# Perceiver layer on one core: V of all groups projected first and loaded back per group, and spare transposes in TensorE's waits

## The chip, the cores and the metric

One Trainium2 chip, one of its cores. The metric is the device time of one execution in microseconds (us), median of several. The engines are TensorE (PE, with its weight loads PEld), VectorE (DVE), ScalarE (ACT), GpSimd (POOL) and SyncE (SP), which here issues all DMAs.

## The reference

```python
# x: 128 x 512 (queries), ctx: 2048 x 512, mask all zeros
xn = layernorm(x)
q = rope((xn @ wq).heads(32)); k = rope((ctx @ wk).heads(8)); v = (ctx @ wv).heads(8)
# query heads 4g..4g+3 share key/value head g
x = x + softmax(q @ k.T / sqrt(128) + mask) @ v  (all heads joined) @ wo
x = x + mamba2(layernorm(x))       # 16 chunks of 512 inner columns, 8 norm groups
x = x + layernorm(x) @ dequant(w).T + bias
```

Only the first stage, cross attention, is rearranged. All data are float32.

## The kernel before

**Three products for one.** Each float32 operand of a large product is kept as a high part (rounded to fp32r) and a low part (the rest), and `pairs` issues three matmuls: high by high, high by low, low by high. ACT mostly makes the high parts (a copy), DVE or POOL the low parts (a subtraction). So each projected block costs a matmul group on TensorE and then one copy and one subtraction elsewhere.

**Groups.** The attention runs in 8 groups of one key/value head and four query heads (`with pe.Fori(0, G - 1)`, the last group written out behind the loop). In the loop body for group g TensorE computes: the scores of g, four heads of four blocks of 512 keys (`scores`); then for group g+1 the K blocks, Q and the first V block (`project_qk_and_first_v`); then `attend`, 16 steps t, each a transposition of the probabilities of 128 keys (`transpose_probs`, one transpose per head) and the product of an earlier step's transposed probabilities with V; then the output projection (`project_out`). The other V blocks of g+1 are placed inside and behind `attend`. A V block is projected as 128 head columns by 512 keys, so it must be copied out of its PSUM bank (`v_copy`) and transposed back by TensorE (`transpose_v_block`, four transposes) before `v_high` and `v_low` split it. That happens 32 times.

**Rotation.** K and Q pass through DVE's `k_rotate` and `q_rotate` (four instructions each: product with the cosine, two half products with the sine, sum), then ACT (`k_high`, `q_high`) and POOL or DVE (`k_low`, `q_low`). The transposed Q lies in `ring_b[0]` (PSUM bank 4) until `q_low` has read it. Step t of `attend` puts its transposes into `ring_b[(t + 1) % 2]`, so step 0 uses bank 5 and step 1 bank 4:

```python
if t == 1 and not last_head:
    pe.wait_ge(s["qT_lo_ready"], g + 2)
if t == 2 and not last_head:
    project_v_block(g + 1, 1)
```

**Order.** It is written by hand: each engine runs its own list and semaphores join them. Each engine's list is in strict order, SP's too. SP issues at the start the context (four blocks of 1 MB), the weights and rope tables of the first group, and the mask; in the loop, per group, `wo`, `wk`, `wv` and `wq`, where `wq` and `wo` share the buffer `wqo_raw` (`wq` of the next-but-one group is issued once `project_out` has finished). ACT splits both `wq` and `wo` (`wq_high`, `wo_high`), POOL subtracts (`wqo_low`). `exps` on ACT makes the probabilities, one instruction of 2048 columns per head, once `mask_scores` on DVE has masked the head's four blocks.

## Time and profile before

| quantity | value |
|---|---|
| median of 3 runs | 738.63 us (735.67 to 745.71) |
| the profiled execution | 734.99 us |
| its span, first to last instruction | 733.1 us |
| mean granted TensorE clock | 0.995 of full speed |

The durations below come from the profiled execution. Its own time is 1.9 us more than its span and 3.6 us under the median. Matmuls overlap in the records (one starts every 0.23 us and is shown with 0.39 us), so work on TensorE is counted from start to start.

### The profile page before, as it was taken

Reading aid. Unit: us, or ns where it says so; the run is one execution under the profiler, and the core shown is the slowest. Engines: PE = TensorE matmul, PEld = TensorE weight load, DVE = VectorE, ACT = ScalarE, POOL = GpSimd, SP = SyncE. Lnnn points to the kernel's source line nnn. Section 1 sums busy time; section 2 is a strip of 40 time slices with the busy share of each in tenths; the row PEclk is TensorE's granted clock in tenths of the full one; section 3 lists DMA queues with packets and bytes.
Section 4 is the critical chain, followed back from the end, with each engine's and each line's share of the span. In section 5 each row is a group of like instructions: output and inputs, shape, how many; then the busy total and the mean of one; then the engine's idle time right before and its main releaser. Section 6 shows DMA issues by size and latency. Waiting matters only on the chain.

```text
span 733.1 us, 11917 instructions
## 1 busy us (share of the span) xinstructions
PE 698.3 (95%) x3929; PEld 594.0 (81%) x3929; DVE 551.2 (75%) x1174; ACT 396.2 (54%) x602; POOL 300.6 (41%) x150
## 2 busy tenths in 40 slices
PE   5899999999999999999999999797979999999996
PEld 4678888888888888888888888686969998999985
DVE  5977658648848857765864874757999889998994
ACT  4364535536446446454553644653776666766752
POOL 3342404404503413230440440200268887888780
PEclk9999999999999999999999999999999999999999
DMA  9601021012001202202101200840897788787700
GB/s 321 244 26 72 1 72 57 14 47 80 16 12 59 72 0 72 72 0 72 57 14 56 72 0 0 316 175 4 311 329 305 285 321 317 294 330 303 276 25 15
DMA packets 20292, 93.74 MB, mean 128 GB/s; under 512 B 2609, under 2 KB 3761, under 8 KB 11441
## 3 DMA queue, kind: packets, MB, share of 16 engines
q1 hardware_dynamic: 20272, 93.50, 34.8%
q8 instruction: 10, 0.16, 0.1%
q14 instruction: 10, 0.07, 0.0%
HBM read 93.17 MB, written 0.33 MB: 128 GB/s over the span
## 4 chain that ended last, share of the span: by engine, by line
PE 87%; DVE 5%; DMA 4%; ACT 2%; issue 1%; SPq 0%; POOL 0%; POOLq 0%; DVEq 0%
PE bank L376 21%; PE bank L378 20%; PE bank L377 20%; PE bank L573 10%; PE bank L486 8%; PE bank L650 3%; PE bank L456 2%; DMA ctx_raw<-in_ctx_t 2%; DMA w_hs_sb<-in_w_hs 1%; DMA wqo_raw<-in_wo 1%; ACT probs L769 1%; PE bank L657 1%; PE bank L624 1%; PE bank L423 1%; DVE decay L1238 1%
## 5 line engine op out<-in xcount | busy, mean ns | idle before, releaser
L1395 POOL TENSOR_TENSOR wqo_lo<-wqo_raw,wqo_hi 128x2048 fp32r<-128x2048 f32 x15 | 69.5, 4632 | 207.1 <-ACT wqo_hi L705 175.6
L1070 DVE TENSOR_TENSOR pt_lo<-bank,pt_hi 128x512 fp32r<-128x512 f32 x128 | 87.7, 690 | 62.2 <-ACT pt_hi L779 62.2
L779 ACT ACTIVATE pt_hi<-bank 128x512 fp32r<-128x512 f32 x128 | 75.7, 598 | 66.0 <-PE bank L486 65.7
L1382 POOL TENSOR_TENSOR k_lo<-rope_a,k_hi 128x512 fp32r<-128x512 f32 x32 | 43.4, 1355 | 105.9 <-ACT k_hi L723 105.9
L1031 DVE CUSTOM_DVE_ANT_0 probs<-bank,mask_sb 128x512 f32<-128x512 f32 x128 | 82.2, 686 | 0.1
L486 PEld LDWEIGHTS bank<-ident,probs 128*128 128x128 f32 x512 | 63.6, 141 | 21.5 <-ACT probs L769 3.7
L486 PE MATMUL bank<-ident,probs 128*128 128x128 f32 x512 | 76.1, 274 | 4.6 <-ACT probs L760 3.3
L1425 POOL TENSOR_TENSOR w_out_lo<-w_out_sb,w_out_hi 128x2048 fp32r<-128x2048 f32 x16 | 73.4, 4587 | 17.2 <-ACT w_out_hi L880 17.2
L1430 POOL TENSOR_TENSOR w_gate_lo<-w_gate_sb,w_gate_hi 128x2048 fp32r<-128x2048 f32 x15 | 69.0, 4597 | 19.2 <-ACT w_gate_hi L872 19.2
L769 ACT ACTIVATE probs<-probs,neg_max 128x2048 f32<-128x2048 f32 x31 | 62.0, 2005 | 1.0 <-DVE neg_max L1021 0.6
L573 PE MATMUL bank<-xnT,w_hs_sb 128*128 128x128 f32 x512 | 59.7, 275 | 0.6 <-DMA w_hs_sb<-in_w_hs 0.6
L376 PE MATMUL bank<-pt_hi,v_hi 128*128 128x512 f32 x128 | 59.4, 464 | 0.0
L573 PEld LDWEIGHTS bank<-xnT,w_hs_sb 128*128 128x128 f32 x512 | 58.4, 192 | 0.8 <-DMA w_hs_sb<-in_w_hs 0.8
L1284 DVE SCALAR_TENSOR_TENSOR conv<-bank,cw,conv 128x127 f32<-128x127 f32 (+2 forms) x192 | 53.6, 341 | 4.3 <-DVE conv L1284 1.8
L723 ACT ACTIVATE k_hi<-rope_a 128x512 fp32r<-128x512 f32 x32 | 20.2, 632 | 64.4 <-DVE rope_a L982 64.4
L376 PE MATMUL bank<-ctx_hi,wk_hi 128*128 128x512 f32 x128 | 51.6, 403 | 1.1 <-DVE ctx_lo L1101 1.1
L376 PE MATMUL bank<-k_hi,qT_hi 128*128 128x512 f32 x128 | 51.4, 401 | 0.0
L376 PE MATMUL bank<-ctx_hi,wv_hi 128*128 128x512 f32 x128 | 51.2, 400 | 0.0
L378 PE MATMUL bank<-ctx_hi,wk_lo 128*128 128x512 f32 x128 | 50.9, 398 | 0.0
L377 PE MATMUL bank<-ctx_lo,wk_hi 128*128 128x512 f32 x128 | 50.8, 397 | 0.0
L378 PE MATMUL bank<-pt_hi,v_lo 128*128 128x512 f32 x128 | 50.7, 396 | 0.0
L377 PE MATMUL bank<-pt_lo,v_hi 128*128 128x512 f32 x128 | 50.4, 394 | 0.0
(186 smaller groups left out, 1709.4 us busy)
## 6 DMA issues: line engine op xcount, KB each, us to landing
w_hs_sb<-in_w_hs SPq DMA_DIRECT2D x16, 1024.0 KB, 4.8
w_gate_sb<-in_w_gate SPq DMA_DIRECT2D x16, 1024.0 KB, 4.8
w_out_sb<-in_w_out SPq DMA_DIRECT2D x16, 1024.0 KB, 6.4
wqo_raw<-in_wq SPq DMA_DIRECT2D x8, 1024.0 KB, 4.8
wqo_raw<-in_wo SPq DMA_DIRECT2D x8, 1024.0 KB, 4.8
decay<-decay_rows SPq DMA_DIRECT2D x16, 512.0 KB, 6.8
ctx_raw<-in_ctx_t SPq DMA_DIRECT2D x3, 1024.0 KB, 11.0
wk_raw<-in_wk SPq DMA_DIRECT2D x8, 256.0 KB, 2.7
```

Of the source, the lines that this page charges most:

```text
L376: pe.matmul(dst, left_hi, right_hi, start=first, stop=False)
L377: pe.matmul(dst, left_hi, right_lo, start=False, stop=False)
L378: return pe.matmul(dst, left_lo, right_hi, start=False, stop=last)
L486: last = pe.transpose(ring_b[(t + 1) % 2][:, h * P:(h + 1) * P], probs[:, h, t * P:(t + 1) * P], ident[:, :])
L573: last = pe.matmul(dst[:, t * P:(t + 1) * P], w[:, c, t * P:(t + 1) * P], xnT[:, c, :], start=c == 0, stop=c == KC - 1)
L769: act.activation(probs[:, h, :], probs[:, h, :], ACT.Exp, bias=neg_max[:, h:h + 1], accum_out=row_sum[:, h:h + 1]).then_inc(s["probs_ready ...
L779: act.activation(pt_hi[t % 3], ring_b[(t + 1) % 2][:, :], ACT.Copy).then_inc(s["pt_hi_ready"], 1)
L1031: dve.tensor_tensor_reduce(out=probs[:, h, b * 512:(b + 1) * 512], in0=ring_a[b][:, :], in1=mask_sb[:, b * 512:(b + 1) * 512], scale=1.0, ...
L1070: dve.tensor_tensor(pt_lo[t % 3], ring_b[(t + 1) % 2][:, :], pt_hi[t % 3].bitcast(F32), ALU.subtract)\
L1395: pool.tensor_tensor(wqo_lo[:, :, :], wqo_raw[:, :, :], wqo_hi[:, :, :].bitcast(F32), ALU.subtract)\
L1425: pool.tensor_tensor(w_out_lo[:, i, :, :], w_out_sb[:, i, :, :], w_out_hi[:, i, :, :].bitcast(F32), ALU.subtract).then_inc(s["wout_lo_read ...
L1430: pool.tensor_tensor(w_gate_lo[:, i, :, :], w_gate_sb[:, i, :, :], w_gate_hi[:, :, :].bitcast(F32), ALU.subtract).then_inc(s["gate_lo_read ...
```

## The change

- **V first.** Before the loop, V of all eight groups is projected as 32 tiles (`project_v`): 128 keys by the columns of four groups, with the context as the stationary operand, so no transposition is needed. The tile goes through ACT (`v_high`) and DVE (`v_low`) into `pt_hi`/`pt_lo`, two slots, and SP stores both parts to DRAM (`store_v`). A slot is free for tile t+2 once its store has landed (`v_out`).
- **V per group.** `load_v` brings 2 MB, high and low, for each group: for group 0 in the middle of the projection, later when the previous group's `attend` has ended. `wv` arrives in two halves of four groups (`wva`, `wvb`), each as four DMAs that write pieces of 128 columns.
- **The loop** loses all V projections, V copies and V transposes. The scores of a group's head 0 move ahead of `project_out` of the group before. K block 3 moves into `attend` at t = 2, its rotation is spread over steps 3, 5, 7 and 9 (`ROPE_STEPS`), and its `k_high` stands behind step 11. The order of the rotation's steps changes: sines first, then the cosine product in PSUM, then a sum that reads PSUM.
- **Splits.** `wo` is split on POOL (`split_wo`) instead of ACT and POOL. `wq_high` of the next group stands behind the first head's exponential.
- **Spare transposes** (`turn_identity`): 32 and 14 at the start, 28 before and 13 behind the last `attend`, 26 and 6 around the second norm, 12, 13 and 12 in the second stage.

```diff
+            for h in range(HG):
+                sp.dma_start(wva_raw[:, :, h * DH:(h + 1) * DH], wv[h]).then_inc(s["wva_in"], 16)
             load_context(1)
...
+            sp.wait_ge(s["ctx_lo_ready"], 4)
+            for h in range(HG):
+                sp.dma_start(wvb_raw[:, :, h * DH:(h + 1) * DH], wv[HG + h]).then_inc(s["wvb_in"], 16)
+
+            def store_v(tile):
+                half, t = tile // KT, tile % KT
+                sp.wait_ge(s["v_lo_ready"], tile + 1)
+                for store, part in zip(v_store, (pt_hi, pt_lo)):
+                    sp.dma_start(store[half, t, :, :], part[tile % 2].bitcast(F32)).then_inc(v_out[tile % 2], 16)
+
+            def load_v(half, h):
+                for store, part in zip(v_store, (v_hi, v_lo)):
+                    sp.dma_start(part[:, :, :].bitcast(F32), store[half, :, :, h * DH:(h + 1) * DH].rearrange("t p d -> p t d"))\
+                        .then_inc(s["v_in"], 16)
...
+                sp.wait_ge(s["pv_ready"], g + 1)
+                load_v((g + 1) // HG, (g + 1) % HG)
+                sp.wait_ge(s["oproj_ready"], g + 1)
+                if g + 2 < G:
+                    sp.dma_start(wqo_raw[:, :, :], wq[g + 2]).then_inc(s["wq_in"], 16)
...
+            def turn_identity(count, spare):
+
+                for _ in range(count):
+                    pe.transpose(spare[:, 0:P], ident[:, :], ident[:, :])
...
+            def project_v(tile):
+                t = tile % KT
+                if tile < KT:
+                    right_hi, right_lo = wva_hi, wva_lo
+                else:
+                    right_hi, right_lo = wvb_hi, wvb_lo
+                    pe.wait_ge(s["wvb_lo_ready"], 1)
+                if tile >= 2:
+                    pe.wait_ge(s["v_lo_ready"], tile - 1)
                 for c in range(KC):
...
+            for b in range(KB):
+                project_k_block(0, b)
+                for t in range(4):
+                    project_v(4 * b + t)
+            for t in range(KT):
+                if t == KT // 2:
+                    project_q(0)
+                if t == 3 * KT // 4:
+                    transpose_q(0)
+                project_v(KT + t)
+            scores(0, range(1))
             with pe.Fori(0, G - 1) as g:
-                scores(g)
-                project_qk_and_first_v(g + 1)
+                scores(g, range(1, HG))
+                project_k_block(g + 1, 0)
+                project_k_block(g + 1, 1)
+                project_q(g + 1)
+                project_k_block(g + 1, 2)
+                transpose_q(g + 1)
                 attend(g, False)
-                transpose_v_block(g + 1, 0)
-                project_v_block(g + 1, 3)
-                transpose_v_block(g + 1, 1)
+                scores(g + 1, range(1))
                 project_out(g)
-                transpose_v_block(g + 1, 2)
-            scores(G - 1)
+            scores(G - 1, range(1, HG))
+            turn_identity(28, bank[4])
             attend(G - 1, True)
+            turn_identity(13, bank[4])
...
+            def v_high(tile):
+                act.wait_ge(s["v_mm"], tile + 1)
+                if tile >= 2:
+                    act.wait_ge(v_out[tile % 2], 32 * (tile // 2))
+                act.activation(pt_hi[tile % 2], v_bank[tile % 2][:, :], ACT.Copy).then_inc(s["v_hi_ready"], 1)
...
             with dve.Fori(0, G - 1) as g:
-                mask_scores(g)
-                q_and_k(g + 1)
+                mask_scores(g, range(1, HG))
+                k_rotate(g + 1, 0)
+                k_rotate(g + 1, 1)
+                q_rotate(g + 1)
+                k_rotate(g + 1, 2)
+                q_low(g + 1)
                 pt_low(g, False)
                 scale_out(g)
-                v_low(g + 1, 0)
                 attn_low(g)
-                v_low(g + 1, 1)
+                mask_scores(g + 1, range(1))
                 add_out(g)
-                v_low(g + 1, 2)
```

**DVE in the loop, between the rotation of Q and the first `pt_lo`.** Bank 7 holds Q, banks 1 and 2 the K blocks 1 and 2, bank 4 the transposed Q. Before:

```order
L991 TENSOR_TENSOR rope_a<-bank7,cos_q 128x512 [waits qproj_ready]
L993 SCALAR_TENSOR_TENSOR rope_b<-bank7,sin_q 128x4x64
L994 TENSOR_TENSOR rope_b<-bank7,sin_q 128x4x64
L996 TENSOR_TENSOR rope_a<-rope_a,rope_b 128x512 [waits qrope_mul]
L969 REGISTER_ALU
L977 TENSOR_TENSOR rope_a<-bank1,cos_k 128x512 [waits qT_mm,kproj_ready]
L978 TENSOR_TENSOR rope_b<-bank1,sin_k 64x512
L979 TENSOR_TENSOR rope_b<-bank1,sin_k 64x512
L982 TENSOR_TENSOR rope_a<-rope_a,rope_b 128x512 [waits krope_mul]
L1001 TENSOR_TENSOR qT_lo<-bank4,qT_hi 128x512 [waits qT_hi_ready]
```

With the change:

```order
L1012 SCALAR_TENSOR_TENSOR rope_b<-bank7,sin_q 128x4x64 [waits k_lo_ready,qproj_ready]
L1013 TENSOR_TENSOR rope_b<-bank7,sin_q 128x4x64
L1015 TENSOR_TENSOR bank7<-bank7,cos_q 128x512 [waits qrope_sin]
L1019 TENSOR_TENSOR rope_a<-bank7,rope_b 128x512 [waits qrope_mul]
L983 REGISTER_ALU
L988 TENSOR_TENSOR rope_b<-bank2,sin_k 64x512 [waits k_lo_ready,kproj_ready]
L990 TENSOR_TENSOR rope_b<-bank2,sin_k 64x512
L994 TENSOR_TENSOR bank2<-bank2,cos_k 128x512 [waits krope_sin]
L998 TENSOR_TENSOR rope_a<-bank2,rope_b 128x512 [waits krope_mul]
L1024 TENSOR_TENSOR qT_lo<-bank4,qT_hi 128x512 [waits qT_hi_ready]
```

The rotation of K block 1 moved ahead of Q's, and the rotation of block 2 now stands between Q's rotation and `qT_lo`.

**TensorE in the loop, at the start of `attend`.** Before, the last matmuls of V block 0 (bank 0) stand in front:

```order
L378 MATMUL bank0<-ctx_hi,wv_lo 128x512
L486 MATMUL bank5<-ident,probs 128x128 [waits v_lo_ready,probs_ready]
L486 MATMUL bank5<-ident,probs 128x128 x3
L486 MATMUL bank4<-ident,probs 128x128 [waits qT_lo_ready]
L486 MATMUL bank4<-ident,probs 128x128 x3
```

With the change:

```order
L417 MATMUL bank2<-ctx_hi,wk_lo 128x512
L464 MATMUL bank4<-ident,rope_a 128x128 [waits qrope_add]
L464 MATMUL bank4<-ident,rope_a 128x128 x3
L500 REGISTER_ALU
L506 MATMUL bank5<-ident,probs 128x128 [waits probs_ready]
L506 MATMUL bank5<-ident,probs 128x128 x3
L506 MATMUL bank4<-ident,probs 128x128 [waits qT_lo_ready]
L506 MATMUL bank4<-ident,probs 128x128 x3
L415 MATMUL bank3<-ctx_hi,wk_hi 128x512 [waits scores_masked]
```

Only the transposes of step 0 stand between the transposes of Q and those that need `qT_lo`; before, K blocks 2 and 3 and V block 0 stood there too.

**SP, in the middle of the V projection**, where the last tile of the first half is stored and V of group 0 loaded. With the change (nothing of this stands before):

```order
L317 DMA v_high<-pt_hi 128x512 [waits v_lo_ready]
L317 DMA v_low<-pt_lo 128x512
L327 DMA wk_raw<-in_wk 128x512 [waits kproj_ready]
L321 DMA v_hi<-v_high 128x16x128 [waits v_out1,v_out0]
L321 DMA v_lo<-v_low 128x16x128
L317 DMA v_high<-pt_hi 128x512 [waits v_lo_ready]
```

The two loads of 1 MB stand in the queue ahead of the next tile's store.

## Rows read from the trace of the kernel before

**Rows 1.** The page: busy time per engine, and the chain that ended last.
```profile
PE 698.3 (95%) x3929; PEld 594.0 (81%) x3929; DVE 551.2 (75%) x1174; ACT 396.2 (54%) x602; POOL 300.6 (41%) x150
...
PE 87%; DVE 5%; DMA 4%; ACT 2%; issue 1%; SPq 0%; POOL 0%; POOLq 0%; DVEq 0%
```
**Rows 2.** Windows (PE, PEld, DVE, ACT, POOL, clock, DMA, GB/s); the second is one loop body.
```profile
24.00:43.00 19.00, 17.93 (x87) 14.83 (x85) 13.65 (x17) 7.24 (x11) 7.62 (x5) 1.00 0.38 144
180.80:240.30 59.50, 59.47 (x304) 49.14 (x303) 41.49 (x86) 29.79 (x41) 18.09 (x11) 1.00 0.14 45
476.00:492.00 16.00, 15.35 (x86) 12.72 (x87) 9.86 (x19) 9.09 (x19) 0.00 (x0) 0.90 0.54 205
506.00:516.00 10.00, 10.00 (x78) 10.00 (x77) 9.10 (x26) 4.25 (x11) 0.00 (x0) 0.83 0.30 88
```
**Rows 3.** Timeline of PE around one V block's transposes (start, duration).
```profile
214.60 0.60 PE L456 MATMUL bank<-ident,rope_b 128*128 128x128 f32 x4
214.96 0.48 PE L376 MATMUL bank<-ctx_hi,wv_hi 128*128 128x512 f32 x1
215.27 0.39 PE L377 MATMUL bank<-ctx_lo,wv_hi 128*128 128x512 f32 x1
```
**Rows 4.** Timeline of PE: first matmul of K block 0, Q and K block 1.
```profile
232.88 0.39 PE L376 MATMUL bank<-ctx_hi,wk_hi 128*128 128x512 f32 x1
...
235.59 0.40 PE L376 MATMUL bank<-wqo_hi,qx_hi 128*128 128x512 f32 x1
...
238.39 0.39 PE L376 MATMUL bank<-ctx_hi,wk_hi 128*128 128x512 f32 x1
```
**Rows 5.** Timeline of DVE, the rotations that follow.
```profile
235.79 0.69 DVE L977 TENSOR_TENSOR rope_a<-bank,cos_k 128x512 f32<-128x512 f32 x1 [1.72 <-PE bank L378]
...
238.59 0.69 DVE L991 TENSOR_TENSOR rope_a<-bank,cos_q 128x512 f32<-128x512 f32 x1
239.20 0.41 DVE L993 SCALAR_TENSOR_TENSOR rope_b<-bank,sin_q 128x256 f32<-128x256 f32 x1
...
244.83 0.68 DVE L1001 TENSOR_TENSOR qT_lo<-bank,qT_hi 128x512 fp32r<-128x512 f32 x1
```
**Rows 6.** Timeline of PE at the start: cold matmuls, and the wait for the first Q.
```profile
9.31 0.63 PE L377 MATMUL bank<-ctx_lo,wk_hi 128*128 128x512 f32 x1
9.74 0.63 PE L378 MATMUL bank<-ctx_hi,wk_lo 128*128 128x512 f32 x1
...
23.55 0.66 PE L423 MATMUL bank<-ident,rope_a 128*128 128x128 f32 x4 [3.46 <-DVE rope_a L996]
```
**Rows 7.** DMA issues: count, size of one, us from issue to landing.
```profile
wqo_raw<-in_wq SPq DMA_DIRECT2D x8, 1024.0 KB, 4.8
wk_raw<-in_wk SPq DMA_DIRECT2D x8, 256.0 KB, 2.7
mask_sb<-in_mask SPq DMA_DIRECT2D x1, 1024.0 KB, 11.8
dtb_bc<-in_dt_bias SPq DMA_DIRECT2D x1, 64.0 KB, 12.1
alog_bc<-in_a_log SPq DMA_DIRECT2D x1, 64.0 KB, 12.8
```
**Rows 8.** Timeline of SP's queue: three issues.
```profile
16.62 0.55 SPq L288 DMA_DIRECT2D mask_sb<-in_mask  x1
...
462.90 0.49 SPq L323 DMA_DIRECT2D dtb_bc<-in_dt_bias  x1
463.43 0.46 SPq L323 DMA_DIRECT2D alog_bc<-in_a_log  x1
```
**Rows 9.** Timeline: ACT and POOL on wq in the loop.
```profile
226.13 1.92 ACT L705 ACTIVATE wqo_hi<-wqo_raw 128x2048 fp32r<-128x2048 f32 x1 [0.66 <-DMA wqo_raw<-in_wq]
...
228.12 4.64 POOL L1395 TENSOR_TENSOR wqo_lo<-wqo_raw,wqo_hi 128x2048 fp32r<-128x2048 f32 x1 [28.11 <-ACT wqo_hi L705]
```
**Rows 10.** Timeline of PE: the last group's wait.
```profile
474.27 1.07 PE L486 MATMUL bank<-ident,probs 128*128 128x128 f32 x8 [3.34 <-ACT probs L760]
```

More of the change, by code:

```diff
@@ L227, in build @@
         same_step_bank = bank[7]
+        v_bank = [bank[5], bank[6]]
+        v_store = [nc.dram_tensor(f"v_{part}", (G // HG, KT, P, HG * DH), F32).ap() for part in ("high", "low")]
         decay_rows = nc.dram_tensor("decay_rows", (CH, HC * P), F32).ap()
@@ new lines, in load_v @@
+            def load_v(half, h):
+                for store, part in zip(v_store, (v_hi, v_lo)):
+                    sp.dma_start(part[:, :, :].bitcast(F32), store[half, :, :, h * DH:(h + 1) * DH].rearrange("t p d -> p t d"))\
+                        .then_inc(s["v_in"], 16)
+            for tile in range(KT):
+                store_v(tile)
+            sp.wait_ge(s["kproj_ready"], KB)
+            sp.dma_start(wk_raw[:, :, :], wk[1]).then_inc(s["wk_in"], 16)
+            for slot in range(2):
+                sp.wait_ge(v_out[slot], 32 * KT // 2)
@@ L462, in scores @@
+            def scores(g, heads):
                 pe.wait_ge(s["qT_lo_ready"], g + 1)
-                for h in range(HG):
+                for h in heads:
                     for b in range(KB):
@@ L645, in chunk_step @@
                     hs_step(1, 0)
+                elif isinstance(n, int) and n == 0:
+                    turn_identity(13, bank[6])
                 pe.wait_ge(s["x_ready"], c + 1)
@@ L654, in chunk_step @@
                     out_step(n + i - 1, 1 - i)
+                if first or last_chunk:
+                    turn_identity(12, bank[1] if last_chunk else bank[3])
                 pe.wait_ge(s["y_gated"], c + 1)
@@ L764, in exps @@
                 for h in range(HG):
+                    if h == 1 and not last_head:
+                        wq_high(g + 1)
                     act.wait_ge(s["neg_max_ready"], HG * g + h + 1)
@@ L783, in pt_high @@
                         act.activation(probs[:, 2, 0:512], oq_bank[:, :], ACT.Copy).then_inc(s["bcast_ready"], 1)
-                if not last_head:
-                    v_copy(g + 1, 1)
+                    if t == 11 and not last_head:
+                        k_high(g + 1, KB - 1)
             def ctx_high(b, pieces=slice(0, KC)):
@@ L797, in _ @@
             ctx_high(0, PAIRS[1])
-            act.wait_ge(s["wq_in"], 16)
-            for two, done in zip(PAIRS, (s["first_wq_hi"], s["wq_hi_ready"])):
-                act.activation(wqo_hi[:, two, :], wqo_raw[:, two, :], ACT.Copy).then_inc(done, 1)
+            act.wait_ge(s["wva_in"], 64)
+            for two in PAIRS:
+                act.activation(wva_hi[:, two, :], wva_raw[:, two, :], ACT.Copy).then_inc(s["wva_hi_ready"], 1)
             act.wait_ge(ctx_in[1], 16)
@@ L1022, in row_max, with mask_scores @@
                     .then_inc(s["neg_max_ready"], 1)
-            def mask_scores(g):
-                for h in range(HG):
+            def mask_scores(g, heads):
+                for h in heads:
                     for b in range(KB):
@@ L1075, in pt_low @@
                         inverse_sums_low(g)
+                    if not last_head and t in ROPE_STEPS:
+                        k_rotate_step(g + 1, KB - 1, ROPE_STEPS.index(t))
             def scale_out(g):
@@ L1120, in _ @@
             ctx_low(1, 3, PAIRS[0])
+            v_low(0)
             ctx_low(1, 4, PAIRS[1])
+            v_low(1)
             first_k_rotate(0)
+            v_low(2)
+            ctx_low(2, 5)
+            v_low(3)
+            v_low(4)
+            first_k_rotate(1)
+            v_low(5)
+            ctx_low(3, 6)
+            for tile in range(6, 9):
+                v_low(tile)
+            first_k_rotate(2)
+            for tile in range(9, 13):
+                v_low(tile)
+            first_k_rotate(3)
@@ L1410, in _ @@
             split_wk(0)
-            split_wv(0)
-            k_low(0)
+            k_low(0, range(1))
+            for c in range(KC):
+                pool.wait_ge(s["wq_hi_ready"], 1)
+                last = pool.tensor_tensor(wqo_lo[:, c, :], wqo_raw[:, c, :], wqo_hi[:, c, :].bitcast(F32), ALU.subtract)
+            last.then_inc(s["wq_lo_ready"], 1)
+            k_low(0, range(1, 2))
+            for c in range(KC):
+                pool.wait_ge(s["wvb_hi_ready"], 1)
+                last = pool.tensor_tensor(wvb_lo[:, c, :], wvb_raw[:, c, :], wvb_hi[:, c, :].bitcast(F32), ALU.subtract)
+            last.then_inc(s["wvb_lo_ready"], 1)
+            k_low(0, range(2, KB))
             with pool.Fori(1, G) as g:
```

330 lines of the change are left out of this document (140 added, 190 removed).

## The prediction

> **What bounds the kernel now.** I read the page first: TensorE is busy for 95% of the span and holds 87% of the chain that ended last [rows 1]. Then the windows: a loop body of one group takes 59.5 us, of which TensorE is busy 59.47 at the full clock, DVE 41.5, ACT 29.8, POOL 18.1; DMA engines are busy 14% [rows 2]. In the loop every matmul taken away counts fully, as long as nobody makes TensorE wait. The timelines then give the prices. The waits outside the loop are few: 3.46 us for the first rotated Q [rows 6], 3.34 us before the last group's transposes [rows 10], and short ones around the norms. I make the sum against the profiled execution's own 734.99 us (span 733.1), which is 3.6 us under the median of 738.63.
>
> **What goes.** The V matmuls do not go: 32 blocks of 12 before, 32 tiles of 12 now, all of 512 columns. They only move ahead of the loop: 12 take 2.71 us from start to start [rows 4]. Only the transposes go. Four of them and the slower start of the next matmul take 215.27 - 214.60 = 0.67 us where one matmul takes 0.23, so 0.44 us per block, and 32 x 0.44 = **-14.1 us** [rows 3]. ACT's copies of V (32) and DVE's and ACT's V splits leave the loop; they were hidden, so they pay nothing by themselves. A loop body without stalls would take 59.5 - 4 x 2.71 - 4 x 0.44 = 46.9 us.
>
> **The start.** The first matmuls run 0.43 us apart against 0.23 later, that is at the 1.2 GHz level; about 14 of them cost 2.8 us, and Q is now needed much later, so the wait of 3.46 us goes as well [rows 6]. Against that the spare transposes (32, then 14) may hold TensorE for longer than the norm does, and V tile 0 must wait for 1 MB more of weights, split by ACT and DVE. I take **-4 us** (0 to -6).
>
> The Trainium skill (TensorE: Matmul & The Clock Gate, "The HAM clock gate") says that the clock rises only with sustained work, which makes spare transposes in a wait useful. The trace agrees in part: the stretch after the 3.34 us wait has a mean granted clock of 0.90, while the stretch behind the 3.46 us wait has 1.00 throughout [rows 2]. By the page alone both long waits would be followed by cold matmuls; the trace shows that a wait of this length sometimes is and sometimes is not.
>
> **Wait A, the first stores.** Tile 2 needs slot 0, which is free when tile 0's store has landed, and TensorE's tile 4 needs `v_lo` of tile 2. The stores stand behind all loads on one queue. Before, the mask landed at 16.6 + 11.8 = 28.4 us [rows 7, 8], and 9 MB were through by then (0.33 MB/us). Now 0.8 MB more come before the mask's end and `wvb` (1 MB) behind it: 28.4 + 5.5 = 34 us, or 39 us if DMAs with pieces of 512 bytes take twice their time (2 MB of them). The store itself lands 2.7 us after it gets its turn, as a load of 256 KB does, and ACT and DVE need 1.4 us. So tile 4 may start at 37 to 42 us. TensorE gets there earlier: tile 0 at about 15, four tiles and K block 1, 5 x 2.71, makes 28.5. The wait is 9 to 13 us, and the next matmuls may start cold (up to 2.8 us): **+13 us**. In steady state a slot needs 0.7 + 0.7, one further issue of 0.5 [rows 8] and 2.7, 4.6 us, and two tiles give it 5.4, so stores are otherwise hidden, by less than a microsecond.
>
> **Wait B, loading V of group 0.** On SP both loads of 1 MB stand between the stores of tiles 15 and 16. Tile 16's store lands later by the loads' time L, and there are about 2 us of slack. What L is, no row shows: the pieces are 512 bytes. Full rate (0.33 MB/us) gives 6 us. The far end is the row of 64 KB loads with 512 bytes per partition: two of them, issued at 462.90 and 463.43, land at 475.0 and 476.2, so 1.2 us for 64 KB and 39 us for 2 MB [rows 7, 8]. That includes each DMA's own overhead, so it is far too dear for two large ones; I stay near the first end and take L = 11 us. Two microseconds of this lie beside the wait for the landing itself. The wait is 1 to 30 us; I take **+5 us**.
>
> The Trainium skill (DMA: Bandwidth & Descriptors, "Specifications") gives 512 bytes as the smallest transfer at line rate. By that rule L is 6 us and the loads cost next to nothing anywhere; no row here shows large transfers in such pieces.
>
> **The loop: a new wait at step 1 of `attend`.** Let K block 0 start at 0. TensorE: K0 to 2.71, K1 to 5.42, Q (2.80) to 8.22, K2 to 10.93, transposes of Q and step 0 (0.44 each) to 11.8, then the transposes of step 1, which overwrite the bank that `qT_lo` reads. DVE: starts 0.20 after K0's end (235.79 - 235.59), at 2.91; a rotation takes 238.59 - 235.79 = 2.80 [rows 4, 5]. K0 to 5.71, K1 to 8.51, Q to 10.7 (two halves at 0.33 and 0.45, two full ones at 0.7), then K2 is only ready at 11.13 and is done at 13.93, and only then `qT_lo` (0.68): 14.6. TensorE goes on at 14.75 instead of 11.8. Before, K blocks 2 and 3 and V block 0 (8.1 us of matmuls) stood in between, and `qT_lo` came ahead of block 2's rotation. So **+2.9 us per group, 7 x 2.9 = +20.3 us** (0 only if DVE ran much faster than in these rows; it has no reason to). In steps 3 to 9 DVE does 1.4 us in some steps of 1.13; the slack of the two-step distance and of K block 3 takes it, with up to 0.5 us per group left over. If TensorE falls to the lower level after the wait, up to 2.4 us per group come on top.
>
> **The loop: wq behind V.** `load_v` is issued when `attend` ends, `wq` 5.5 us later behind it on the queue. From `attend`'s end to the next Q are 2.71 + 2.80 + 3 x 2.71 + 2 x 2.71 = 19.1 us. `wq` needs, from its turn, 2.7 to 4.8 us to land, 1.9 on ACT and 4.6 on POOL [rows 7, 9]: about 10. So L may be 9 us before Q waits; at 11 it waits 2 us, and every further microsecond counts seven times. ACT waits for `wq` too, with the exponentials of heads 1 to 3 (6 us) and then `k_high` behind it, which gives the same delay or a little more. I take **+1.5 us per group, +10.5 us** (0 to 90). The other queued work has room: `wo` on POOL (a copy and a subtraction of 4.6 us) is done long before `project_out`; `attn_lo` follows the last product by three operations of 0.7 us, and the scores of head 0 cover 2.7.
>
> **The end.** Exponentials of the last group no longer stand behind `wo`'s copy, so 3.34 us shrink, but 28 spare transposes (0.11 each, 3.1 us) fill the same place: about -0.3. The clock stays up there (0.90 over 16 us before, so 3.2 us at the lower level) and behind the second norm (0.83 over 10 us, 3.4 us at it); half of each is lost time [rows 2]. The other spare transposes fit waits of their length. **-3.5 us** (-4 to +2).
>
> **Sum:** -14.1 - 4 + 13 + 5 + 20.3 + 10.5 - 3.5 = +27.2. 734.99 + 27 = **762 us**.
>
> **The rivals.**
> 1. *DMA is hidden, the DVE wait is not.* Pieces of 512 bytes run at full rate, A is 9 us, B 1, wq 0: -14.1 - 4 + 9 + 1 + 20.3 - 3.5 = +8.7, 744 us. For it: the DMA engines idle for 86% of a loop body [rows 2]. Against: the stores' landing time bounds A whatever the rate.
> 2. *Faster.* Both long new waits are absent or mostly covered: the stores overtake the backlog, and DVE reaches `qT_lo` in time. Then -14.1 - 4 + 1 + 0 + 2 - 3.5 = -18.6, 716 us. For it: TensorE is the bound and really loses work. Against: the order on DVE, and one queue for all.
> 3. *V's loads are slow.* L = 15 to 20: Q waits 6 to 11 us per group, B grows to 10: 762 + 7 x 4.5 + 5 = 799 us and up to 840. This decides from L = 9 us on. For it: the 1.2 us rows. Against: they price small DMAs.
> 4. *The spare transposes do nothing* beyond their place (the waits were too short to cool the engine): only the -3.5 and part of the start go, +5 us on any of these.
>
> **How the numbers follow.** My case, both waits with L around 11: 0.40, 750 to 785. Rival 1: 0.25. Rival 2: 0.18. Rival 3: 0.17. Faster or slower by over 2% is about what a measurement of this kernel tells from no change: below 724 or above 753 us. Rival 2 is mostly below; of rival 1 most is within 2% and some above; my case is above but for a tenth, rival 3 all above. Faster 0.16, same 0.25, slower 0.59. The range leaves out the upper part of rival 3 and the lower of rival 2: 717 to 800.
>
> **What would show it.** Right: no `L456` work and TensorE's V matmuls in one stretch of about 90 us; a PE idle of 9 us or more between tiles 3 and 4, at 28 to 40 us, released by `pt_lo`; the waits table with seven waits of some 2.9 us of the transposes for `qT_lo`; loop periods of 50 to 52 us; DMA writes of 16 MB. Wrong: periods under 48 us (DVE was in time), or the V stretch under 92 us from tile 0 to tile 31 (stores never held it); periods over 54 us with ACT waiting for `wqo_raw` is rival 3.

## The result: 771.33 us, 4.4% slower

Before takes 740.17 us (median of 4 runs beside the new one, 735.67 to 745.71), the changed kernel 771.33 us (4 runs, 768.93 to 772.12). The ratio is 1.0435, 95% interval 1.0387 to 1.0484. The prediction of 762 us has the side right and is 9 us short. Its sum was made against the profiled execution of 734.99 us; the profiled one of after takes 770.9 us, span 769.2. So the trace has +36 us to explain where the sum had +27.

The page of after, in the same order as [rows 1], with the line of the granted clock in 40 slices between:

```profile
PE 719.1 (93%) x3957; PEld 606.8 (79%) x3957; DVE 547.5 (71%) x1174; ACT 368.2 (48%) x564; POOL 308.5 (40%) x150
...
PEclk9889999999999999999999999999999999999999
...
PE 68%; issue 14%; DVE 8%; DMA 3%; POOL 3%; SPq 2%; ACT 1%; POOLq 0%; DVEq 0%; ACTq 0%
```

TensorE is busy 20.8 us longer than before. The transposes of V that are gone (19.0 us in the table of groups) and the 156 turns that came (21.1 us) nearly cancel, so the same matmuls ran slower. TensorE's part of the chain that ended last fell from 87% to 68%. DVE, POOL and SP's queue gained 2 to 3 points each, and most of the rest is "issue", time for which the page names no wait, so the shares alone don't say who is to blame. The waits of PE, in total, times and longest:

```profile
PE bank L506 <- DVE qT_lo L1024: 18.7, 7, 2.7
PE bank L415 <- DVE pt_lo L1030: 16.5, 5, 9.4
...
PE bank L415 <- DVE wva_lo L1133: 1.3, 1, 1.3
```

These are the two kinds that the prediction named: seven times `qT_lo` in the loop, and in the V stretch five for `pt_lo`, which there is the low part of a V tile. The windows of after, with the columns of [rows 2]: the matmuls behind the first long wait, then two loop bodies, then the stretch around the wait inside the second of them.

```profile
39.30:44.60 5.30, 5.28 (x12) 4.13 (x13) 2.77 (x2) 2.28 (x2) 2.95 (x3) 0.50 0.52 198
...
159.90:211.70 51.80, 48.99 (x239) 39.50 (x238) 38.34 (x81) 23.45 (x32) 18.07 (x9) 0.97 0.28 86
211.70:263.00 51.30, 48.62 (x239) 39.58 (x238) 38.25 (x81) 23.46 (x32) 18.07 (x9) 0.97 0.28 86
...
211.70:220.30 8.60, 5.93 (x26) 4.78 (x25) 5.76 (x11) 2.31 (x4) 4.71 (x3) 0.80 0.19 82
```

The granted clock is 0.97 in each loop body, and the last row shows where it is lost: in the 8.6 us around the wait it is 0.80, and in the other 42.7 us of that body it is 1.00. A loop body takes 51.8 us the first time and 51.3 on average later, against 59.5 before [rows 2]. The prediction had 46.9 for one without stalls. PE in the second of them:

```profile
211.72 0.60 PE L464 MATMUL bank<-ident,rope_a 128*128 128x128 f32 x4
212.16 0.60 PE L506 MATMUL bank<-ident,probs 128*128 128x128 f32 x4
215.42 1.11 PE L506 MATMUL bank<-ident,probs 128*128 128x128 f32 x4 [2.67 <-DVE qT_lo L1024]
216.19 0.77 PE L415 MATMUL bank<-ctx_hi,wk_hi 128*128 128x512 f32 x1
216.76 0.63 PE L416 MATMUL bank<-ctx_lo,wk_hi 128*128 128x512 f32 x1
217.19 0.63 PE L417 MATMUL bank<-ctx_hi,wk_lo 128*128 128x512 f32 x1
...
218.89 0.40 PE L415 MATMUL bank<-ctx_hi,wk_hi 128*128 128x512 f32 x1
...
220.28 0.60 PE L506 MATMUL bank<-ident,probs 128*128 128x128 f32 x4
```

Three things are to be read here. The wait is 2.67 us. Behind it the starts lie 0.43 us apart (216.76, 217.19), which is the 1.2 GHz level, until 218.9; at 2.4 GHz they lie 0.23 apart [rows 4]. And step 2 starts 4.86 us after step 1, where four transposes and K block 3 need 3.26 at the full clock (run c). From the first group to the last this distance shrinks from 4.83 and 4.86 to 4.62. DVE in the same stretch shows why the wait is there:

```profile
211.92 0.69 DVE L988 TENSOR_TENSOR rope_b<-bank,sin_k 64x512 f32<-64x512 f32 x1 [0.45 <-PE bank L417]
...
214.08 0.69 DVE L998 TENSOR_TENSOR rope_a<-bank,rope_b 128x512 f32<-128x512 f32 x1
214.69 0.68 DVE L1024 TENSOR_TENSOR qT_lo<-bank,qT_hi 128x512 fp32r<-128x512 f32 x1
```

Four operations of K block 2's rotation, two of them in the part left out, stand ahead of `qT_lo`. ACT had its input ready at 212.96.

The V stretch. SP's queue (issue and its duration), then ACT, which has to wait for the slot, then PE:

```profile
21.23 9.37 SPq L311 DMA_DIRECT2D wvb_raw<-in_wv  x4
30.65 2.44 SPq L317 DMA_DIRECT2D v_high<-pt_hi  x1
```

```profile
37.95 0.60 ACT L753 ACTIVATE pt_hi<-bank 128x512 fp32r<-128x512 f32 x1 [8.42 <-DMA v_low<-pt_lo]
```

```profile
39.32 0.79 PE L415 MATMUL bank<-wva_hi,ctx_hi 128*128 128x512 f32 x1 [9.36 <-DVE pt_lo L1030]
...
99.52 0.76 PE L415 MATMUL bank<-wvb_hi,ctx_hi 128*128 128x512 f32 x1 [5.01 <-DVE pt_lo L1030]
100.08 0.63 PE L416 MATMUL bank<-wvb_lo,ctx_hi 128*128 128x512 f32 x1
100.50 0.63 PE L417 MATMUL bank<-wvb_hi,ctx_lo 128*128 128x512 f32 x1
```

The first row is tile 4, the second tile 20. The loads of V, which had no row before, and `wq` beside [rows 7]:

```profile
wqo_raw<-in_wq SPq DMA_DIRECT2D x8, 1024.0 KB, 6.4
v_high<-pt_hi SPq DMA_DIRECT2D x32, 256.0 KB, 2.1
v_low<-pt_lo SPq DMA_DIRECT2D x32, 256.0 KB, 2.4
v_hi<-v_high SPq DMA_DIRECT2D x8, 1024.0 KB, 5.8
v_lo<-v_low SPq DMA_DIRECT2D x8, 1024.0 KB, 9.1
```

`wq` is in time, but only just. ACT waits for its landing, POOL's subtraction follows, and Q's first matmul follows that. The first round, then POOL in the second:

```profile
199.37 1.92 ACT L732 ACTIVATE wqo_hi<-wqo_raw 128x2048 fp32r<-128x2048 f32 x1 [2.69 <-DMA wqo_raw<-in_wq]
201.37 4.64 POOL L1427 TENSOR_TENSOR wqo_lo<-wqo_raw,wqo_hi 128x2048 fp32r<-128x2048 f32 x1 [17.07 <-ACT wqo_hi L732]
206.07 0.50 PE L415 MATMUL bank<-wqo_hi,qx_hi 128*128 128x512 f32 x1
...
252.51 4.63 POOL L1427 TENSOR_TENSOR wqo_lo<-wqo_raw,wqo_hi 128x2048 fp32r<-128x2048 f32 x1 [16.38 <-ACT wqo_hi L732]
```

In the first round POOL ends at 206.01 and Q starts at 206.07, 0.28 us later than the matmuls ahead of it would allow. In the second POOL ends at 257.14 and Q starts on time at 257.58. In the later rounds the margin is 0.25 to 0.54 us.

The last group's wait of [rows 10] is filled with turns and then over:

```profile
508.42 3.22 PE L422 MATMUL bank<-ident 128*128 128x128 f32 x28
511.47 1.04 PE L506 MATMUL bank<-ident,probs 128*128 128x128 f32 x8
```

### The profile page after: what moved, and what is told of

Same layout as the page of the kernel before. It is cut to its first block, busy times and chain, and to the rows that moved or that the text cites. A ratio compares the mean times of both kernels' runs of the same rounds, so it can differ in the third digit from the quotient of the medians.

```text
span 769.2 us, 11882 instructions
## 1 busy us (share of the span) xinstructions
PE 719.1 (93%) x3957; PEld 606.8 (79%) x3957; DVE 547.5 (71%) x1174; ACT 368.2 (48%) x564; POOL 308.5 (40%) x150
## 3 DMA queue, kind: packets, MB, share of 16 engines
q1 hardware_dynamic: 65584, 127.06, 46.9%
## 4 chain that ended last, share of the span: by engine, by line
PE 68%; issue 14%; DVE 8%; DMA 3%; POOL 3%; SPq 2%; ACT 1%; POOLq 0%; DVEq 0%; ACTq 0%
PE bank L415 16%; PE bank L416 15%; PE bank L417 15%; PE bank L596 9%; PE bank L506 7%; PE bank L675 3%; POOL wqo_lo L1427 1%; SPq L311 1%; DMA w_hs_sb<-in_w_hs 1%; DMA wva_raw<-in_wv 1%; PE bank L422 1%; DVE bank L994 1%; DVE rope_b L990 1%; DVE rope_b L988 1%; PE bank L684 1%
## 5 line engine op out<-in xcount | busy, mean ns | idle before, releaser
L1083 DVE TENSOR_TENSOR pt_lo<-bank,pt_hi 128x512 fp32r<-128x512 f32 x128 | 87.9, 691 | 57.7 <-ACT pt_hi L780 57.3
L780 ACT ACTIVATE pt_hi<-bank 128x512 fp32r<-128x512 f32 x128 | 76.4, 597 | 84.6 <-PE bank L506 84.2
L1414 POOL TENSOR_TENSOR k_lo<-rope_a,k_hi 128x512 fp32r<-128x512 f32 x32 | 41.2, 1287 | 159.8 <-ACT k_hi L746 159.8
L506 PE MATMUL bank<-ident,probs 128*128 128x128 f32 x512 | 80.5, 281 | 20.1 <-DVE qT_lo L1024 18.7
L1427 POOL TENSOR_TENSOR wqo_lo<-wqo_raw,wqo_hi 128x2048 fp32r<-128x2048 f32 x7 | 32.5, 4639 | 157.6 <-ACT wqo_hi L732 157.6
L506 PEld LDWEIGHTS bank<-ident,probs 128*128 128x128 f32 x512 | 63.4, 144 | 39.2 <-DVE qT_lo L1024 20.3
L1030 DVE TENSOR_TENSOR pt_lo<-bank,pt_hi 128x512 fp32r<-128x512 f32 x32 | 22.1, 691 | 78.0 <-ACT pt_hi L753 78.0
L753 ACT ACTIVATE pt_hi<-bank 128x512 fp32r<-128x512 f32 x32 | 19.1, 596 | 75.8 <-PE bank L417 51.5
L415 PE MATMUL bank<-ctx_hi,wk_hi 128*128 128x512 f32 x128 | 54.5, 426 | 0.9 <-DVE ctx_lo L1116 0.8
L416 PE MATMUL bank<-ctx_lo,wk_hi 128*128 128x512 f32 x128 | 53.3, 416 | 0.0
L416 PE MATMUL bank<-k_lo,qT_hi 128*128 128x512 f32 x128 | 50.0, 390 | 0.0
```

The lines of the kernel that those rows point to most:

```text
L415: pe.matmul(dst, left_hi, right_hi, start=first, stop=False)
L416: pe.matmul(dst, left_hi, right_lo, start=False, stop=False)
L506: last = pe.transpose(ring_b[(t + 1) % 2][:, h * P:(h + 1) * P], probs[:, h, t * P:(t + 1) * P], ident[:, :])
L780: act.activation(pt_hi[t % 3], ring_b[(t + 1) % 2][:, :], ACT.Copy).then_inc(s["pt_hi_ready"], 1)
L1083: dve.tensor_tensor(pt_lo[t % 3], ring_b[(t + 1) % 2][:, :], pt_hi[t % 3].bitcast(F32), ALU.subtract)\
```

## The experiments

Each median is to be held against after (771.33) or before (about 740); each ratio is to the runs of before on the same chip, with its 95% interval.

### a. `qT_lo` ahead of K block 2's rotation

```diff
                 q_rotate(g + 1)
+                q_low(g + 1)
                 k_rotate(g + 1, 2)
-                q_low(g + 1)
                 pt_low(g, False)
```

> One edit in VectorE's loop: qT_lo is made ahead of the rotation of K block 2. With K block 0 started at 0, Q is rotated at about 10.9 us, transposed at 11.4, copied by ACT at 12.1 and qT_lo is done at about 12.9, where TensorE arrives at 11.8: the wait of 2.67 us shrinks to about 1.1. Theory (each of the seven waits costs its own 2.67 us and then about 2.2 us at the lower clock): if a wait of 1.1 us doesn't lower the clock, the period falls from 51.8 to about 48.0 us and the kernel to about 744 us; if it does, to about 50.2 us and 760 us. Rival (the lower clock after the wait is no loss of its own, the period is set by DVE anyway): only 1.6 us per group go, 760 us at a full clock.

Measured: 758.7 us, 1.0295 (1.0221 to 1.037). PE in its second group:

```profile
214.66 0.66 PE L506 MATMUL bank<-ident,probs 128*128 128x128 f32 x4 [0.97 <-DVE qT_lo L1024]
...
219.50 0.63 PE L506 MATMUL bank<-ident,probs 128*128 128x128 f32 x4 [1.44 <-DVE pt_lo L1083]
```

The wait fell to 0.97 us as computed, and the clock stayed up (K block 3's starts are 0.23 apart). But the rotation, moved behind, delayed `pt_lo` of step 0, and step 2 now waits 1.44 us. The period is 49.8 us. So neither figure of the theory was met by its own way: 12.6 us came back rather than 27, because the work that stood in the way had only changed its place. The rival's number (760 us at a full clock) fits, and so does half of its reason: DVE still holds TensorE for 0.97 + 1.44 = 2.41 us per group where it was 2.67. Its other half, that the lower clock costs nothing, doesn't fit: the waits lost 0.26 us per group and the period 1.5. Run c tests that by itself.

### b. K block 3 ahead of step 1

```diff
                     if t == 1 and not last_head:
+                        project_k_block(g + 1, KB - 1)
                         pe.wait_ge(s["qT_lo_ready"], g + 2)
-                    if t == 2 and not last_head:
-                        project_k_block(g + 1, KB - 1)
```

> One edit on TensorE: K block 3 is projected ahead of step 1 of attend instead of ahead of step 2. Its 2.71 us stand where the wait of 2.67 us was. Theory: the wait goes altogether and with it the lower clock behind it; step 2 may wait 0.3 us for pt_lo of step 0. Period 46.9 to 47.4 us, 7 x 4.6 = 32 us less than 770.9: 737 to 742 us. Rival (DVE is what holds the group: its work, 38 us of a period, is delayed by the same amount wherever TensorE waits): the wait moves to step 2 or 3, the period stays above 50 us, 758 us or more.

Measured: 747.33 us, 1.0151 (1.0068 to 1.0234).

```profile
212.96 0.66 PE L506 MATMUL bank<-ident,probs 128*128 128x128 f32 x4
214.32 0.63 PE L506 MATMUL bank<-ident,probs 128*128 128x128 f32 x4 [0.71 <-DVE pt_lo L1082]
```

Step 1 no longer waits, the clock is full, 0.71 us of waiting is left at step 2, and the period is 48.0 us. One order on one engine is worth 24 us. The theory's mechanism holds, its size was 5 us too good: 0.71 us of waiting where it had 0.3, a body without stalls that takes 47.2 us and not 46.9 (run c), and in the first round a Q 0.93 us late for `wq`, whose margin went with the longer wait.

### c. The wait kept, but filled

```diff
                     if t == 1 and not last_head:
+                        turn_identity(23, oq_bank)
                         pe.wait_ge(s["qT_lo_ready"], g + 2)
```

> The wait for qT_lo stays, but TensorE fills it with 23 turns of the identity (2.6 us). Theory (of the 4.9 us that a group takes over its unstalled 46.9, 2.67 are the wait and 2.2 the lower clock after it): the period falls from 51.8 to about 49.6 us, the kernel to about 755 us, and the mean granted clock of a period rises from 0.97 to 1.00. Rival (the lower clock costs nothing of its own, since DVE paces the steps after the wait): period 51.8 us, 771 us, unchanged though the clock is full.

Measured: 759.37 us, 1.0304 (1.0229 to 1.0379).

```profile
212.60 2.67 PE L422 MATMUL bank<-ident 128*128 128x128 f32 x23
215.43 0.66 PE L506 MATMUL bank<-ident,probs 128*128 128x128 f32 x4 [0.15 <-DVE qT_lo L1025]
...
218.69 0.60 PE L506 MATMUL bank<-ident,probs 128*128 128x128 f32 x4
```

Compare with the rows of after above. Step 1 starts at 215.43 here and 215.42 there, so DVE holds it just as long. Step 2 follows after 3.26 us here and 4.86 there: in this group 1.60 us are the lower clock and nothing else. In the seven groups of after the excess over 3.26 is 1.57, 1.60, 1.49, 1.42, 1.37, 1.36 and 1.36 us, 10.2 in all. The spans of the two profiled executions differ by 10.3 us, the medians by 12.0. The rival is out. The theory's 2.2 us per group was too much, as a body without stalls takes 47.2 us: 49.9 here less the 2.7 that the turns fill, or 51.3 - 2.67 - 1.44 in after.

### d. No turns at all

```diff
-                for _ in range(count):
+                for _ in range(0):
```

> All turns of the identity left out (they feed no result). From the profiles of before and after, the tail from the last scores to the end took 262.2 us before and 260.8 now, and the start some 2.8 us less. Theory: the turns at the start save about 2.8 us of the lower clock, those in the tail 1.4 us, and elsewhere nothing: 775 us. Rival 4 of the prediction (they do nothing): 771 us; a third reading, that they themselves delay the work behind them: below 770 us.

Measured: 771.25 us, 1.0498 (1.0406 to 1.059), by the medians the same as after. The start shows where the gain goes. PE, K block 0 and V tile 0 without turns:

```profile
10.90 0.76 PE L415 MATMUL bank<-ctx_hi,wk_hi 128*128 128x512 f32 x1 [3.50 <-DVE ctx_lo L1116]
...
16.16 0.48 PE L415 MATMUL bank<-wva_hi,ctx_hi 128*128 128x512 f32 x1
```

and with them, in after:

```profile
11.07 0.47 PE L415 MATMUL bank<-ctx_hi,wk_hi 128*128 128x512 f32 x1 [0.83 <-DVE ctx_lo L1116]
...
15.70 0.50 PE L415 MATMUL bank<-wva_hi,ctx_hi 128*128 128x512 f32 x1 [1.33 <-DVE wva_lo L1133]
```

With the turns K block 0 runs at the full clock, and TensorE then waits 1.33 us for the weights of V. Tile 4 starts at 39.07 without and 39.32 with them: the first store decides, not the clock. In the profiled executions the turns are worth 0.8 us by the rotated Q of group 1 (159.91 with, 160.75 without) and 0.4 us behind the last loop body, and against that the first wait for `qT_lo` was followed by the full clock without the turns (1.6 us) and by the lower clock with them. So rival 4 of the prediction holds for this kernel to within a microsecond or two.

### e. First stores ahead of the second half's weights

```diff
-            sp.wait_ge(s["ctx_lo_ready"], 4)
-            for h in range(HG):
-                sp.dma_start(wvb_raw[:, :, h * DH:(h + 1) * DH], wv[HG + h]).then_inc(s["wvb_in"], 16)
...
             for tile in range(KT):
                 store_v(tile)
+                if tile in (2, 4, 6, 8):
+                    h = tile // 2 - 1
+                    sp.dma_start(wvb_raw[:, :, h * DH:(h + 1) * DH], wv[HG + h]).then_inc(s["wvb_in"], 16)
```

ACT's copy of `wvb` moves behind tile 11, POOL's subtraction behind K block 2.

> The four loads of wvb (9.4 us of issue in the profile of after) are taken from their place ahead of the first store of V and issued one by one behind the stores of tiles 2, 4, 6 and 8; ACT and POOL split wvb later to match. Theory (the first store is late because it is issued behind these loads): the store of tile 0 is issued at about 22 us, lands at 25 to 29, and TensorE's wait of 9.36 us ahead of tile 4 with the 2.5 us of lower clock behind it shrinks to 0 to 2 us: 10 to 12 us less, 759 to 762 us. Rival (it is the backlog of bytes of context, tables and mask that holds the store, not the issues behind it): the store lands at 33 us or later, the wait is 5 us or more, 766 us or more.

Measured: 766.88 us, 1.0357 (1.0272 to 1.0443).

```profile
20.29 0.53 SPq L314 DMA_DIRECT2D v_high<-pt_hi  x1
```

```profile
34.10 0.60 ACT L753 ACTIVATE pt_hi<-bank 128x512 fp32r<-128x512 f32 x1 [5.48 <-DMA v_low<-pt_lo]
```

```profile
35.48 0.80 PE L415 MATMUL bank<-wva_hi,ctx_hi 128*128 128x512 f32 x1 [6.41 <-DVE pt_lo L1031]
```

The store is issued 10.4 us earlier than in after and lands only 3.9 us earlier, 13.2 us after the issue of its second half. Its bytes stand in the queue behind context, tables and mask. The rival is right in the main: about 6.4 of the 9.4 us are the backlog, 3 are `wvb`. The median fell by 4.5 us, 1.5 more than the wait shrank. In the profiled execution the first wait for `qT_lo` was followed by the full clock here too, which is worth 1.6 us; whether that is so in the other runs is not on record.

### f. V of group 0 loaded behind the last store

```diff
-            for slot in range(2):
-                sp.wait_ge(v_out[slot], 32 * KT // 2)
-            load_v(0, 0)
             for tile in range(KT, 2 * KT):
                 store_v(tile)
...
             for slot in range(2):
                 sp.wait_ge(v_out[slot], 32 * KT)
+            load_v(0, 0)
```

> V of group 0 is loaded behind the last store of V instead of between the stores of tiles 15 and 16. Theory (the store of tile 16 lands late because two loads of 1 MB stand ahead of it): the wait of 5.01 us ahead of tile 18 falls to below 1 us, with the 1.7 us of lower clock behind it, and the load lands some 10 us after the last store, at about 150, well before step 2 of attend at 166: 6 us less, 765 us. Rival (the wait comes from the state of the queue, or the load is needed earlier): unchanged at 771 us, or a new wait for v_hi at step 2.

Measured: 760.34 us, 1.0291 (1.0205 to 1.0377). (The expectation names tile 18; the wait is ahead of tile 20.) PE's waits for the low part of V:

```profile
PE bank L413 <- DVE pt_lo L1028: 11.9, 4, 9.7
```

The 5.01 us are gone, and there is no wait for `v_hi`. By the rotated Q of group 1 this kernel is 8.8 us ahead of after (151.14 against 159.91). Of these 2.0 are there by tile 7 (48.97 against 50.98), where the two kernels are still the same, so 6.8 belong to wait B: its 5.01 and the 1.7 of slow matmuls behind it. By group 2 it is 10.7 us ahead, since `wq` of the first round no longer comes 0.28 us late and the first wait of the loop was followed by no lower clock (1.00 over the first round). The whole is 11 us, of which wait B is the larger part and not all.

### g. The turns alone, in the kernel before

The same turns at the same places of the kernel before (the 28 in `pv_bank`), and nothing else.

> The kernel before with nothing of the V change, only with the turns of the identity at the same places (32, 14, 28, 13, 26, 6, 13, 12 and 12). Theory (they keep the clock up where TensorE waits, but what comes behind waits for data anyway): the start saves up to 2.8 us, the tail up to 1.4: 0 to 4 us less, ratio 0.995 to 1.000. Rival: all of the lower clock of these stretches is real loss and comes back, 5 us or more, ratio 0.993 or less.

Measured: 734.88 us, 0.9937 (0.9897 to 0.9977). In the kernel before the turns bring 5 us, 0.6%, and the interval lies below 1. The ratio lies between the theory's (0.995 or more) and the rival's (0.993 or less), nearer the rival's, and the interval covers both. The granted clocks on record point at the same cause: their median is 0.995 over these ten runs and 0.988 over the thirteen of before beside them. At half speed where it is low, 0.7% of 735 us is an estimate of 5 us. In which stretches they arise isn't settled: the profiled execution took 737.66 us, 2.7 more than that of before, and so does not show them.

### h. `wq` ahead of V in the queue

```diff
-                sp.wait_ge(s["pv_ready"], g + 1)
-                load_v((g + 1) // HG, (g + 1) % HG)
                 sp.wait_ge(s["oproj_ready"], g + 1)
                 if g + 2 < G:
                     sp.dma_start(wqo_raw[:, :, :], wq[g + 2]).then_inc(s["wq_in"], 16)
+                sp.wait_ge(s["pv_ready"], g + 1)
+                load_v((g + 1) // HG, (g + 1) % HG)
```

on top of b.

> K block 3 ahead of step 1 as in the run b_k3_early, and on the queue wq of the next group ahead of the loads of V. Theory (the wait of 0.77 us of Q for wqo_lo there is the load of V ahead of wq, the prediction's term of +1.5 us per group, hidden only behind the longer wait in after): it goes, 7 x 0.7 = 5 us less than b_k3_early, 742 us; V's load then lands later, still before step 2. Rival (wq is bound by its own issue after project_out, ACT and POOL, not by the load ahead of it): the same 747 us.

Measured: 748.93 us, 1.0128 (1.0047 to 1.0209), the same as b. The wait of 0.77 us that the expectation speaks of came once in b, in the first round, and not seven times; here it is gone, and the period is 48.0 us in both. The load of V ahead of `wq` takes that one wait and otherwise only margin: ACT's idle time for `wq` falls from 13.4 us in b to 4.6.

### k. Edits b, e and f together

> K block 3 ahead of step 1, stores of V ahead of the wvb loads, and V of group 0 loaded behind the last store, together. Theory (the three losses are independent, and only the wait behind the backlog of loads is left): from 771.3, minus 24.0, 4.5 and 11.0 as measured alone, gives 732 us, ratio about 0.99. Rival (they share a cause, one wait moves into another's place): 740 us or more.

Measured: 736.22 us, 0.9965 (0.9933 to 0.9998). 35 us of the expected 39.5 came back. Part of the difference is probably counted twice in the expectation: the profiled executions of e and f each had a first round without the lower clock (1.6 us), and b takes that lower clock away as well. So the losses are nearly independent.

### j. k, with the first four stores on ACT's queue

```diff
             v_high(0)
+            store_first_v(0)
```

and so behind tiles 1 to 3, where `store_first_v(t)` waits for `v_lo_ready` and issues both stores with `act.dma_start`.

> As k_three_edits, but the stores of tiles 0 to 3 are issued by ACT on its own queue instead of by SP behind the loads of context, tables and mask. Theory (these stores wait in SP's queue for the bytes ahead of them): they land about 3 us after their issue at 20 us, the wait of 6.4 us ahead of tile 4 shrinks to 2 us or less and with it 1.7 to 2.5 us of lower clock: 6 to 8 us under k_three_edits, 724 to 726 us. Rival (the DMA engines themselves are full until 33 us, whichever queue asks): the wait stays at 5 to 6 us, and the time within 2 us of k_three_edits.

Measured: 734.02 us, 0.9928 (0.9901 to 0.9954). PE's waits in the V stretch, here and then in k:

```profile
PE bank L416 <- DVE pt_lo L1040: 5.8, 6, 1.7
```

```profile
PE bank L413 <- DVE pt_lo L1028: 8.7, 4, 6.5
```

The longest wait shrank from 6.5 to 1.7 us, without a lower clock behind it, and group 2 is reached 4.0 us earlier (194.58 against 198.55). The rest then took 1.4 us more, and the medians differ by 2.2, with intervals that overlap. The store of tile 1 still took over 8 us here (issued at 25.13 and 25.49, ACT goes on at 34.15), so a queue of its own shortens the way past a backlog and does not remove it. The DMA engines were full: their share is 0.96 or more until 36 us.

The Trainium skill (DMA: Bandwidth & Descriptors, "Queues, rings and completion order") says that each DMA engine serves the queues that have work in turn, packet by packet, and each queue's ring in order. Both halves agree with e and j: 13.2 us behind the backlog in SP's queue, and under 9 us (34.15 - 25.49) beside it.

### l. ACT copies step 0 ahead of K block 2

```diff
                 q_high(g + 1)
-                k_high(g + 1, 2)
                 pt_high(g, False)
...
+                    if t == 0 and not last_head:
+                        k_high(g + 1, 2)
```

on top of j.

> j_act_queue with one edit on ACT: the probabilities of step 0 are copied ahead of the last copy of K block 2 instead of behind it. In b_k3_early DVE waited 0.58 us for that copy, and TensorE 0.71 us for pt_lo at step 2. Theory (this order is what is late there): the seven waits of 0.71 us go, the period falls from 48.0 to about 47.4 us, 4 us less than j_act_queue: 730 us. Rival (DVE reaches pt_lo late anyway, behind the rotation of K block 2): the wait stays, 734 us.

Measured: 733.66 us, 0.9934 (0.9899 to 0.9968), the same as j.

```profile
202.67 0.66 PE L507 MATMUL bank<-ident,probs 128*128 128x128 f32 x4 [0.33 <-DVE pt_lo L1094]
```

Steps 1 and 2 start without a wait, and step 4 waits 0.33 us instead. The period is 48.0 (48.2 in j). Neither reading is quite right: the order on ACT was what step 2 waited for, but removing it pays nothing. TensorE now waits for DVE's `pt_lo` two steps later; DVE has `pt_lo`, the inverse sums, the diagonals and a rotation in the first steps, and that it is the slower one there was not tried by itself. The time is the rival's.

### m. Three slots for V tiles

Tiles 0 to 23 take turns in three slots, the third being `qT_hi` and `qT_lo`; the rest is l.

> l_act_order with three slots instead of two for V tiles on their way to memory (the third is the place of qT_hi and qT_lo, free until tile 24). Theory (each tile waits for the landing of the store two tiles back, with less than 1 us of slack): the six waits for pt_lo in the V stretch, 5.8 us in all in j_act_queue, go: 4 to 6 us less than l_act_order, 725 us, ratio about 0.98. Rival (what holds the tiles is the split on ACT and DVE beside context and K, not the landing): within 1 us of l_act_order.

Measured: 732.7 us, 0.9904 (0.9869 to 0.9939).

```profile
PE bank L428 <- DVE qT_lo L1054: 2.6, 2, 1.7
PE bank L428 <- DVE pt_lo L1054: 2.5, 3, 1.0
```

The median is 1.0 us under l's. Two of seven waits of l are gone and 5.1 of 6.9 us remain, so it is mostly the rival: what holds these tiles is not the landing. A rotation of K on DVE stands between the low parts of two tiles in the code; that it is this is likely and wasn't tried by itself.

## Why the prediction was right, and what it lacked

**The sum, term by term.**

| term | predicted | found | from |
|---|---|---|---|
| V transposes gone | -14.1 | -12.0 | a body without stalls takes 47.2 (run c), predicted 46.9: 7 x 0.3 less |
| start | -4 | -3.4 | K0 2.3 later, 2.4 of lower clock and Q's 3.46 gone, 1.3 for V's weights, 1.1 for `v_lo` gone |
| wait A | +13 | +11.9 | 9.36, and 2.56 at the lower clock |
| wait B | +5 | +6.7 | 5.01, and 1.7 at the lower clock |
| wait for `qT_lo` | +20.3 | +18.7 | 7 x 2.67 |
| lower clock behind it | 0 | +10.2 | 1.60 falling to 1.36 per group (run c) |
| `wq` behind V | +10.5 | +0.3 | first round only |
| short waits, slower tiles | 0 | +3.5 | three waits of 0.7; 16 tiles at 2.81 instead of 2.72 |
| end | -3.5 | -1.4 | last scores to end 262.2 before, 260.8 after |
| sum | +27.2 | +34.5 | the trace has +36.1; 1.6 us stay unassigned |

**The new wait on DVE** was right in place, count and cause, and nearly in size. Runs a, b and c show it from three sides: move the cause, cover the wait, fill the wait. Of the signs that the prediction named, the idle time of 9 us or more between tiles 3 and 4 came (9.36), the seven waits came (2.67 each), and the period lies between 50 and 52 us.

**The step that failed** is the sentence "If TensorE falls to the lower level after the wait, up to 2.4 us per group come on top", which the sum took at nothing. It does fall, in all seven groups; by run c it costs 1.36 to 1.60 us per group, 10.2 in all. The prediction had left it open because in before one wait of 3.34 us was followed by slow matmuls and one of 3.46 was not [rows 2]. Here 2.67 us were followed by it seven times in seven, with only transposes just ahead of and behind the wait; in the first rounds of d, e and f the same wait was not. What decides is not shown.

**The term that was too dear** is `wq` behind V: 10.5 us for 0.3. L was taken as 11 us between ends of 6 and 39. The two loads of group 0 are issued at 87.5 and 87.9, and by the medians of 5.8 and 9.1 us both are in after about 9.5. In the first round of the loop it was 10.1. The prediction's rule had Q wait from L = 9 on. It was about 1 us too strict: `wq` lands 2.4 us behind V, where the rule's sum of about 10 us took it in the middle of 2.7 to 4.8. So Q is late by 0.28 us once and on time by 0.25 to 0.54 us otherwise. The term was near its edge and not far from it, and by these margins a load of V slower by 1 us would have cost in every round. These two misses, +10.2 and -10.2, cancel, and that the forecast came within 9 us owes much to that: it is luck. The 9 us themselves are small terms: short waits and slower tiles (3.5), the transposes (2.1), the end (2.1), B (1.7), the start (0.6) and the unassigned 1.6, less A and `qT_lo` (2.7).

The prediction cited the Trainium skill (DMA: Bandwidth & Descriptors, "Specifications"), by which pieces of 512 bytes go at line rate; L would then be 6 us, an estimate from the 0.33 MB/us of the start. The 9.5 us lie nearer to that than to the dear end, but not on it.

**Wait A** was as forecast (39.3 us for a start at 37 to 42). What was not clear is its make-up, and the expectation of run e put it on the wrong part: two thirds are bytes queued earlier, a third the loads of `wvb`.

**The rivals.** Rival 1 (744) had DMA hidden and the DVE wait real: true of `wq` and of the length of wait A (9 us, measured 9.36), too low on B (1 us for 5.01), and, like my case, without the slow matmuls in the loop. Rival 2 (faster) is what runs k to m turn the kernel into: with the three losses taken away it is 0.4 to 1.0% faster than before, far from the rival's 716 us. Rival 3 did not happen. Rival 4 held for this kernel within a microsecond or two, and in the kernel before the turns were worth 5 us.

**Where the gain of the idea went.** Of the 14.1 us of transposes 12.0 were really saved. The best version (m, 732.7) is 7 us under before, and the turns alone (g) are 5 us under it. So of V's move little is left even when it is repaired: the period is 48.0 us where 47.2 would be without stalls, 6 us in seven groups, and 5 us of waits in the V stretch come on top. No run has the repaired order without the turns, so how the 7 us divide between V's move and the turns is not shown.

## What to carry to other kernels

When work leaves a loop or changes its place, look at what it covered: here K blocks 2 and 3 and V block 0, 8.1 us of matmuls, gave DVE time to finish `qT_lo`, and without them in that place a chain that had been hidden cost more (18.7 us of waits and 10.2 of slow matmuls) than the work saved (12.0). Price a new wait on TensorE twice, once for its length and once for the slow matmuls behind it, and if the wait can't go, put other matmuls into it (24 us here) before turns of the identity (12 us). And a store issued behind a backlog of loads on one queue waits for their bytes, wherever its own issue stands.
